# Two halves for projections and four-tile turns on TensorE in an attention and expert kernel

## The chip, the cores and the metric

The kernel runs on one core of a Trainium2 chip. The metric is device time in microseconds (us) for one execution, the median of several runs. TensorE's queue is called PE below, its weight loads PEld, VectorE DVE, ScalarE ACT, GpSimd POOL and SyncE SP. ACTq and SPq are rows of DMAs that those two queues issue.

## The reference, cut to what matters

```python
# x: 16 batches x 512 tokens x 128 channels; 16 heads of 8 channels
h = layernorm(x) * (1 + ca) + sa
Q, K, V = h @ Wq.T, h @ Wk.T, h @ Wv.T      # reshaped to (16 heads, batch, 512, 8) over the flat data
atten = softmax(Q K^T)                       # 512 x 512 for each batch and head
y = atten V + h
x = x + ga * (y - mean(y)) / sqrt(var(y) + eps)      # mean and variance over a whole batch
h = layernorm(x) * (1 + cb) + sb
x = x + gb * experts(h)                      # 8 experts of 128 -> 256 -> 128, the best two by a gate
```

## The kernel before, in words

Attention comes first, in 17 stages (`over_stages`), then the expert layer, batch by batch (`f_batch`). Each engine has its own instruction queue with the order written out by hand, and the queues meet on semaphores.

A stage has 16 quads (`r`), each with four heads (`h`). In a quad PE issues, for each head, one score matmul of pass A (`pass_a`, L1135, keys across a row, for the row maxima) and one of pass B (`pass_b`, L1147, transposed scores, for the exponentials); A and B of one head lie on different halves of the array's rows and run as a pair. The quad ends with the value matmuls (`values`, L1160, eight instructions, since each f32 matmul is issued as two). Pass A runs on batch b. Pass B and the values run 13 quads (`LAG`) behind it, so that in the first 13 quads of stage b they work on batch b-1. DVE takes the row maxima of pass A (L716), ACT the exponentials of pass B (L985). Passes A and B have three PSUM banks each: a pass-A matmul waits for the maximum three before it, a pass-B matmul for the exponential three before it.

One more PSUM bank, `misc`, serves all the other work on PE, one use after the other. `misc_uses(b)` lists by quad what stage b does there: quad 0 the turn (transpose) of the next batch's normed input (`x_turn`), quad 1 the row maxima of the batch before (`max_rows`), quads 2, 3 and 4 the next batch's projections `q`, `k`, `v`, quads 8 to 10 two one-column matmuls and another `max_rows`, quad 15 the turn of an earlier batch's result (`z_turn`). PE does such a use in `fill`, behind the second head (`h == 1`) of the quad: it waits on `s_misc_read` until the use before has been read, issues the matmuls, and counts up `s_misc_full`. ACT reads the bank (`evacuate`: L932 hT, L937 q_f, L941 k_f, L945 v_f, L949 max_rows) before the exponentials of the next quad; DVE reads `z_turn` (L763) behind the maxima of quad 15. In quad 2, ACT also issues three DMAs between its second and third exponential (`halfway`: two at L974, one at L999).

The projections go through memory before the next stage can use them. POOL splits q_f, then k_f, into three bf16 parts (lines 339 to 345). SP, in a fixed order, stores q (L373) and v (L382), loads Qt (L393), stores k (L378), loads v (L421) and loads Kt (L411). The first pass-A matmul of the next stage waits on `s_q_landed` and `s_k_landed`.

Stage 0 has pass A alone in its first 13 quads. Stages 0 to 14 do x_turn, q, k and v for the next batch; stages 2 to 16 do z_turn. Stage 16 has no pass A. Before stage 0 the first batch's four fills run by themselves, and the last batch's end is done among the experts (`end_piece`).

Of the kernel before, what the change touches and what calls it, by code (L numbers as in the profile page):

```python
# [15 lines left out]
P = 128  # L16
# [18 lines left out]
TT = S // P  # L35
# [27 lines left out]
def misc_index(what, b, g=0):  # L63

    return MISC[(what, b, g)]
# [7 lines left out]
def build(nc, x, wqT, wkT, wvT, w1, b1T, w2, b2T, w3, b3, gate_w, cT, wmod, out):  # L73
    ctx = ExitStack()
    with ctx:
        def sb(name, shape, dt=F32):
            return ctx.enter_context(nc.sbuf_tensor(name, shape, dt))

        def sem(name):
            return ctx.enter_context(nc.semaphore(name))  # L80
# [49 lines left out]
        hT = sb("hT", [P, S])  # L130
# [77 lines left out]
        misc = bank[7]  # L208
        misc_bf = misc[:].bitcast(BF16)

        def end_bank(b):

            return pv_bank if isinstance(b, int) and b == NB - 1 else misc
# [21 lines left out]
        s_misc_full = sem("s_misc_full")  # L235
# [86 lines left out]
        def has(b, first, last):  # L322

            return not isinstance(b, int) or first <= b <= last
# [756 lines left out]
        def _(pe):  # L1081
# [4 lines left out]
            for j in range(6):  # L1086
                ins = pe.matmul(misc[:, j * NB:(j + 1) * NB], wmod_sb[:, j], c_silu[:], start=True, stop=True)
# [2 lines left out]
            pe.transpose(misc[0:NB, 0:D], mod[:, 5], ident[:]).then_inc(s_gb_mm, 1)  # L1090
            pe.wait_ge(s_gb, 1)

            def fill(what, b, g=0):

                n = misc_index(what, b, g)
                if n:
                    pe.wait_ge(s_misc_read, n)
                if what == "x_turn":
                    pe.wait_ge(s_x_norm, TT * (b + 1))
                    for t in range(TT):  # L1100
                        ins = pe.transpose(misc[:, P * t:P * t + P], x_norm[:, t], ident[:])
                if what in ("q", "k"):
                    w = wq_sb if what == "q" else wk_sb
                    ins = pe.matmul(misc[:], w[:], hT[:], start=True, stop=True)  # L1104
                if what == "v":
                    for t in range(TT):
                        ins = pe.matmul(misc[:, P * t:P * t + P], hT[:, P * t:P * t + P], wv_sb[:],  # L1107
                                        start=True, stop=True)
                if what == "max_rows":
                    pe.wait_ge(s_split_max[3], 2 * b + g + 1)  # L1110
                    ins = pe.transpose(misc_bf[0:PARTS * MCOLS, 0:P], max_parts[:].rearrange("p a i n -> p (a i n)"),
                                       ident_bf[:])
                if what == "mean":
                    pe.wait_ge(s_y_mv, b + 1)
                    ins = pe.matmul(end_bank(b)[:, 0:1], mean_mat[:], y_mv[:, 0:1], start=True, stop=True)
                if what == "var":
                    pe.wait_ge(s_y_sq, b + 1)
                    ins = pe.matmul(end_bank(b)[:, 0:1], mean_mat[:], y_sq[:], start=True, stop=True)
                if what == "z_turn":
                    pe.wait_ge(s_z, b + 1)  # L1120
                    for t in range(TT):
                        ins = pe.transpose(end_bank(b)[:, P * t:P * t + P], z[:, P * t:P * t + P], ident[:])
                ins.then_inc(s_misc_full, 1)

            def pass_a(b, r, h):
                g, c = r // 4, r % 4
                a, n = head(g, h)
                first = HALF * a
                m = b * STEPS + 4 * r + h
                if r + h == 0:  # L1130
                    pe.wait_ge(s_q_landed, (b + 1) * LOADS * DMA)
                    pe.wait_ge(s_k_landed, (b + 1) * LOADS * DMA)
                if m >= 3:
                    pe.wait_ge(s_max, m - 2)
                pe.matmul(score_a[m % 3][:], Qt[b % BUFS][first:first + ROWS, n, P * c:P * c + P],  # L1135
                          Kt[b % BUFS][first:first + ROWS, n], start=True, stop=True).then_inc(s_a, 1)
# [58 lines left out]
            def stage(b, par):  # L1195
                for r in range(QUADS):
                    for h in range(4):
                        if has(b, 0, NB - 1):
                            pass_a(b, r, h)
                        if r < LAG and has(b, 1, NB):  # L1200
                            pass_b(b - 1, r + QUADS - LAG, h)
                        if r >= LAG and has(b, 0, NB - 1):
                            pass_b(b, r - LAG, h)
                        if h == 1:
                            for q, what, ub, g in misc_uses(b):
                                if q == r:
                                    fill(what, ub, g)
                    if r <= LAG and has(b, 1, NB):
                        values(b - 1, 1 - par, r + QUADS - LAG - 1)
                    if r > LAG and has(b, 0, NB - 1):  # L1210
                        values(b, par, r - LAG - 1)
                    if b_is(b, NB) and 1 <= r <= E:
                        f_piece(0, 0, r - 1)
# [84 lines left out]
```

## Time and profile before

| | |
|---|---|
| median of 3 runs | 1527.62 us (1523.94 to 1529.97) |
| profiled execution, its own time | 1535.74 us |
| its span | 1533.9 us |
| mean granted TensorE clock, share of full speed | 0.973 |
| busy: PE, DVE, ACT, POOL | 88%, 75%, 56%, 18% |
| stage 0, from its first pass A | 52.1 to 98.6 us |
| stages 1 to 14 | 98.6 to 808.1 us |
| stages 15 and 16 | 808.1 us to about 893 us |
| experts | from about 893 us |

All rows come from one execution. A start in a row is in us from the span's start. The idle time in brackets is what the engine spent before that instruction, and the name behind the arrow is the inferred releaser; "issue" means that the profile shows none, which is also what a wait for a DMA can look like. Matmuls overlap, so their step is read from one start to the next and not from the duration.

### The profile page before, as it was taken

To read this page: it belongs to the slowest core of one execution; us is meant where nothing else is said; L and a number is where in the kernel's file an instruction comes from. 1 tells how busy PE (TensorE), PEld (TensorE's weight loads), DVE (VectorE), ACT (ScalarE), POOL (GpSimd) and SP (SyncE) were. 2 spreads that over 40 slices of the span, in tenths; PEclk is the share of its full clock that TensorE was granted. 3 is DMA by queue.
4 is the path that set the end of the run, shared out by engine and by line. 5 is a ranking of instruction groups with operands and counts; after the bars stand their busy time and mean duration, and the time that the engine had idled before them with its cause. 6 is when DMAs were issued, how large, how long until landed. Compare 5 with 4: busy or idle time off the path is not lost.

```text
span 1533.9 us, 24345 instructions
## 1 busy us (share of the span) xinstructions
PE 1355.0 (88%) x8445; PEld 735.2 (48%) x8445; DVE 1151.3 (75%) x2821; ACT 855.6 (56%) x1590; POOL 279.8 (18%) x411
## 2 busy tenths in 40 slices
PE   2697888888878888888888899999999999999998
PEld 1121222122212222222221258888888888888887
DVE  4587888898888888887898437766676766677775
ACT  2067787788887787877787753333333333333332
POOL 3221332233213331332121111000000000000000
PEclk9999999999999999999999799999999999999999
DMA  8346465556555565646552210000000000000000
GB/s 157 78 76 121 89 127 116 105 119 128 121 112 122 116 131 114 118 107 125 110 112 64 75 44 23 16 16 17 16 16 16 16 16 16 17 16 14 11 11 13
DMA packets 355834, 108.93 MB, mean 71 GB/s; under 512 B 282448, under 2 KB 338176, under 8 KB 352640
## 3 DMA queue, kind: packets, MB, share of 16 engines
q1 hardware_dynamic: 343232, 89.81, 29.9%
q10 hardware_dynamic: 12480, 17.57, 3.8%
q8 instruction: 67, 1.10, 0.3%
q14 instruction: 55, 0.45, 0.1%
HBM read 59.88 MB, written 46.67 MB: 69 GB/s over the span
## 4 chain that ended last, share of the span: by engine, by line
PE 65%; DVE 18%; ACT 9%; issue 4%; ACTq 3%; DMA 1%; SPq 1%; POOL 0%; POOLq 0%; DVEq 0%
PE bank L1231 22%; PE bank L1243 15%; DVE neg_max L716 14%; PE bank L1160 10%; PE bank L1135 7%; ACT probs L985 5%; PE bank L1147 4%; ACTq L974 2%; PE bank L1104 2%; PE bank L1107 1%; DMA Kt<-k_dram 1%; PE bank L1191 1%; ACTq L999 1%; PE bank L1180 1%; ACT x_norm L959 1%
## 5 line engine op out<-in xcount | busy, mean ns | idle before, releaser
L716 DVE TENSOR_REDUCE neg_max<-bank 128x1 f32<-128x512 f32 x1024 | 638.3, 682 | 134.3 <-PE bank L1135 132.0
L985 ACT ACTIVATE probs<-bank 128x512 f32<-128x512 f32 x1024 | 539.7, 603 | 165.9 <-PE bank L1147 156.1
L1135 PE MATMUL bank<-Kt,Qt 48*128 48x512 bf16 x1024 | 346.5, 407 | 105.3 <-DVE neg_max L716 56.6
L1231 PE MATMUL bank<-h_part,w_parts 128*128 128x512 f32 x1536 | 384.3, 399 | 3.3 <-DVE hidden L881 3.3
L1066 ACT ACTIVATE gate_act<-bank,b_sb 128x512 f32<-128x512 f32 x256 | 176.4, 689 | 373.8 <-PE bank L1231 373.7
L1147 PE MATMUL bank<-Qt,Kt 51*128 51x512 bf16 x1024 | 339.4, 401 | 25.1 <-ACT probs L985 24.0
L1231 PEld LDWEIGHTS bank<-h_part,w_parts 128*128 128x128 f32 x1536 | 278.2, 188 | 64.8 <-DVE hidden L881 10.2
L881 DVE SCALAR_TENSOR_TENSOR hidden<-bank,b_sb,gate_act 128x512 f32<-128x512 f32 x256 | 190.7, 750 | 136.9 <-ACT gate_act L1066 136.4
L1135 PEld LDWEIGHTS bank<-Kt,Qt 48*128 48x128 bf16 x1024 | 73.9, 95 | 455.9 <-DVE neg_max L716 364.2
L1160 PE MATMUL bank<-probs,Vt 128*16 128x512 f32 x2048 | 282.2, 624 | 0.1
L1243 PEld LDWEIGHTS bank<-w_sb,hidden 128*128 128x128 f32 x2048 | 247.1, 192 | 8.9
L1243 PE MATMUL bank<-w_sb,hidden 128*128 128x128 f32 x2048 | 249.0, 275 | 0.0
L892 DVE SCALAR_TENSOR_TENSOR acc<-bank,w_dense,acc 128x128 f32<-128x128 f32 x512 | 144.0, 344 | 45.0 <-PE bank L1243 44.9
L1147 PEld LDWEIGHTS bank<-Qt,Kt 51*128 51x128 bf16 x1024 | 73.0, 94 | 70.2 <-ACT probs L985 67.6
L648 POOL TENSOR_TENSOR y_out<-acc,gb_all 128x512 f32<-128x512 f32 x16 | 20.6, 1289 | 445.9 <-DVE acc L892 445.9
L1160 PEld LDWEIGHTS bank<-probs,Vt 128*16 128x16 f32 x2048 | 33.6, 95 | 76.0 <-issue 50.9
L339 POOL CAST max_parts<-neg_max 128x32 bf16<-128x32 f32 x32 | 6.8, 211 | 311.3 <-DVE neg_max L716 311.3
L994 ACT ACTIVATE o_sb<-bank 128x512 f32<-128x512 f32 x64 | 38.2, 597 | 12.9 <-PE bank L1160 12.0
L339 POOL CAST q_parts<-q_f 128x512 bf16<-128x512 f32 x15 | 9.2, 616 | 146.6 <-ACT q_f L937 146.6
L610 POOL TENSOR_TENSOR f_rstd<-f_ve,neg_half 128x4 f32<-128x4 f32 x16 | 16.3, 1016 | 98.6 <-DVE f_ve L690 98.6
L959 ACT ACTIVATE x_norm<-x_in,x_shift,x_rstd 128x128 f32<-128x128 f32 x64 | 27.9, 492 | 10.9 <-DVE x_shift L702 10.9
L586 POOL TENSOR_TENSOR x_rstd<-x_ve,neg_half 128x4 f32<-128x4 f32 x16 | 16.3, 1020 | 90.2 <-DVE x_ve L690 90.2
(123 smaller groups left out, 797.7 us busy)
## 6 DMA issues: line engine op xcount, KB each, us to landing
o_dram<-o_sb ACTq DMA_DIRECT2D x64, 256.0 KB, 3.9
q_dram<-q_parts SPq DMA_DIRECT2D x48, 128.0 KB, 4.5
k_dram<-k_parts SPq DMA_DIRECT2D x48, 128.0 KB, 11.6
Qt<-q_dram SPq DMA_DIRECT2D x32, 192.0 KB
Kt<-k_dram SPq DMA_DIRECT2D x32, 192.0 KB
x_in<-in_x SPq DMA_DIRECT2D x16, 256.0 KB, 3.1
h_dram<-hT SPq DMA_DIRECT2D x16, 256.0 KB, 3.7
Qt<-q_dram SPq DMA_DIRECT2D x32, 128.0 KB
```

The lines of the kernel that those rows point to most:

```text
L716: dve.tensor_reduce(neg_max[:, side, a, col:col + 1], score_a[m % 3][:], AX_X, ALU.max, negate=True).then_inc(s_max, 1)
L881: dve.scalar_tensor_tensor(hidden[slot], up_bank[2 * c + 1][:], b2_sb[:, c, e:e + 1], gate_act[:, c], ALU.add, ALU.mult).then_inc(s_hid, 1)
L892: ins = dve.scalar_tensor_tensor(acc[:, par, t], down_bank[e % 2][:, P * t:P * t + P], w_dense[par][:, t, e:e + 1], acc[:, par, t], ALU.mu ...
L959: act.activation(x_norm[:, t], x_in[:, t], ACT.Identity, bias=x_shift[:, t:t + 1], scale=x_rstd[:, t:t + 1]).then_inc(s_x_norm, 1)
L985: act.activation(probs[:, 4 * (j % 2) + (k ^ 1)], score_b[n % 3][:], ACT.Exp).then_inc(s_exp, 1)
L994: act.activation(o_sb[:, g % 2], pv_bank[:], ACT.Copy).then_inc(s_o, 1)
L1066: act.activation(gate_act[:, c], up_bank[2 * c][:], ACT.Silu, bias=b1_sb[:, c, e:e + 1])\
L1135: pe.matmul(score_a[m % 3][:], Qt[b % BUFS][first:first + ROWS, n, P * c:P * c + P], Kt[b % BUFS][first:first + ROWS, n], start=True, stop ...
L1147: pe.matmul(score_b[m % 3][:], Kt[b % BUFS][first:first + ROWS + PARTS, n, P * c:P * c + P], Qt[b % BUFS][first:first + ROWS + PARTS, n], ...
L1160: ins = pe.matmul(pv_bank[32 * h:32 * h + 2 * DK, :], Vt[:, par, 4 * (N8 * a + n) + c], probs[:, 4 * (j % 2) + h], start=(c == 0), stop=(c ...
L1231: ins = pe.matmul(up_bank[2 * c + k][:], w[:, i, e, P * c:P * c + P], h_parts[par][j], start=(i + j == 0), stop=(i == 1))
L1243: ins = pe.matmul(down_bank[e % 2][:, P * t:P * t + P], hidden[HC * (e % 2) + c][:, P * t:P * t + P], w3_sb[:, e, c], start=(c == 0), stop ...
```

## The change

`fill` gets a parameter `half`. For x_turn, q, k, v and z_turn (`h_turn` is named too and is no use of this kernel) it is called twice: behind the quad's second head with half 0, and behind its fourth head, ahead of the value matmuls, with half 1. A half is two of the four tiles, or 256 of the 512 columns of the q and k projections. The wait on `s_misc_read` stands in front of the first half only and `s_misc_full` is counted behind the second half only. The waits for the normed input and for z stand in front of both. `max_rows` and the one-column matmuls stay whole, and calls outside the stages have no halves.

```diff
+            def in_two(what):
+                return what in ("x_turn", "q", "k", "v", "z_turn", "h_turn")
+
-            def fill(what, b, g=0):
+            def fill(what, b, g=0, half=None):
 
+                tiles = range(TT) if half is None else range(TT // 2 * half, TT // 2 * (half + 1))
+                columns = slice(P * tiles[0], P * tiles[-1] + P)
                 n = misc_index(what, b, g)
-                if n:
+                if n and not half:
                     pe.wait_ge(s_misc_read, n)
                 if what == "x_turn":
                     pe.wait_ge(s_x_norm, TT * (b + 1))
-                    for t in range(TT):
+                    for t in tiles:
                         ins = pe.transpose(misc[:, P * t:P * t + P], x_norm[:, t], ident[:])
                 if what in ("q", "k"):
                     w = wq_sb if what == "q" else wk_sb
-                    ins = pe.matmul(misc[:], w[:], hT[:], start=True, stop=True)
+                    ins = pe.matmul(misc[:, columns], w[:], hT[:, columns], start=True, stop=True)
                 if what == "v":
-                    for t in range(TT):
+                    for t in tiles:
                         ins = pe.matmul(misc[:, P * t:P * t + P], hT[:, P * t:P * t + P], wv_sb[:],
                                         start=True, stop=True)
...
-                    for t in range(TT):
+                    for t in tiles:
                         ins = pe.transpose(end_bank(b)[:, P * t:P * t + P], z[:, P * t:P * t + P], ident[:])
-                ins.then_inc(s_misc_full, 1)
+                if half != 0:
+                    ins.then_inc(s_misc_full, 1)
...
-                        if h == 1:
+                        if h in (1, 3):
                             for q, what, ub, g in misc_uses(b):
-                                if q == r:
+                                if q == r and in_two(what):
+                                    fill(what, ub, g, h // 2)
+                                elif q == r and h == 1:
                                     fill(what, ub, g)
```

## Rows read from the trace of the kernel before

**Rows 1.** Timeline of PE, first pass A of four stages: start, us, line [idle].
```profile
403.18 0.37 PE L1135 MATMUL bank<-Kt,Qt 48*128 48x512 bf16 x1 [1.05 <-issue]
...
602.73 0.37 PE L1135 MATMUL bank<-Kt,Qt 48*128 48x512 bf16 x1 [1.66 <-issue]
...
652.73 0.37 PE L1135 MATMUL bank<-Kt,Qt 48*128 48x512 bf16 x1 [1.89 <-issue]
...
705.01 0.58 PE L1135 MATMUL bank<-Kt,Qt 48*128 48x512 bf16 x1 [2.34 <-issue]
```
**Rows 2.** Windows: stretch, us, then PE, PEld, DVE, ACT, POOL busy, PEclk, DMA share, GB/s.
```profile
96.00:97.00 1.00, 1.00 (x6) 0.15 (x2) 0.50 (x1) 0.40 (x1) 0.00 (x0) 1.00 0.24 40
...
402.00:403.00 1.00, 0.13 (x4) 0.00 (x0) 0.85 (x2) 0.17 (x1) 0.53 (x3) 1.00 0.35 88
403.00:404.00 1.00, 0.82 (x7) 0.43 (x8) 0.34 (x1) 0.32 (x1) 0.92 (x3) 1.00 0.01 2
```
**Rows 3.** Timeline of the SP queue in the stage that began at 602.73.
```profile
616.60 3.28 SPq L373 DMA_DIRECT2D q_dram<-q_parts  x3
...
643.18 2.14 SPq L411 DMA_DIRECT2D Kt<-k_dram  x6
```
**Rows 4.** Timeline of ACT, the reading of q in three of those stages.
```profile
412.31 0.60 ACT L937 ACTIVATE q_f<-bank 128x512 f32<-128x512 f32 x1
...
612.14 0.60 ACT L937 ACTIVATE q_f<-bank 128x512 f32<-128x512 f32 x1
...
663.97 0.60 ACT L937 ACTIVATE q_f<-bank 128x512 f32<-128x512 f32 x1
```
**Rows 5.** Timeline of all engines, quads 0 to 2 of the stage that began at 403.18.
```profile
403.68 2.17 ACT L985 ACTIVATE probs<-bank 128x512 f32<-128x512 f32 x4 [1.52 <-PE bank L1147]
...
405.74 0.78 ACT L932 ACTIVATE hT<-bank,mod 128x512 f32<-128x512 f32 x1
...
406.06 0.38 PE L1135 MATMUL bank<-Kt,Qt 48*128 48x512 bf16 x1
...
406.40 2.07 ACT L985 ACTIVATE probs<-bank 128x512 f32<-128x512 f32 x4
...
406.57 0.12 PEld L1111 LDWEIGHTS bank<-ident_bf,max_parts 128*96 128x96 bf16 x1 [0.63 <-ACT hT L932]
...
408.99 0.26 ACT L949 ACTIVATE max_rows<-bank 96x128 bf16<-96x128 bf16 x1
...
410.85 0.44 ACTq L999 DMA_DIRECT2D o_dram<-o_sb  x1
...
411.34 1.09 ACT L985 ACTIVATE probs<-bank 128x512 f32<-128x512 f32 x2 [1.11 <-PE bank L1147]
```
**Rows 6.** Groups by line and form, 300 to 800 us: count, busy us, mean ns.
```profile
L1104 PE MATMUL bank<-hT,wq_sb 128*128 128x512 f32 x20 | 11.3, 644 | 3.4 <-ACT max_rows L949 3.4
```
**Rows 7.** Windows, four us from the start of two of the stages (columns of Rows 2).
```profile
652.73:656.73 4.00, 4.00 (x20) 0.96 (x20) 2.58 (x4) 2.84 (x5) 0.00 (x1) 0.59 0.06 8
...
403.18:407.18 4.00, 3.86 (x29) 1.33 (x29) 3.41 (x6) 3.50 (x7) 0.80 (x2) 1.00 0.08 12
```
**Rows 8.** Timeline of stage 0, quad 2, the q projection.
```profile
58.00 2.07 PE L1104 MATMUL bank<-hT,wq_sb 128*128 128x512 f32 x2
...
60.64 2.48 DVE L716 TENSOR_REDUCE neg_max<-bank 128x1 f32<-128x512 f32 x4 [1.44 <-PE bank L1135]
```
**Rows 9.** Timeline of PE, second head of quad 4 up to the values.
```profile
720.17 0.38 PE L1135 MATMUL bank<-Kt,Qt 48*128 48x512 bf16 x1
720.50 1.16 PE L1107 MATMUL bank<-wv_sb,hT 128*128 128x128 f32 x8
721.59 0.39 PE L1135 MATMUL bank<-Kt,Qt 48*128 48x512 bf16 x1
...
721.82 0.38 PE L1135 MATMUL bank<-Kt,Qt 48*128 48x512 bf16 x1
722.13 1.05 PE L1160 MATMUL bank<-probs,Vt 128*16 128x512 f32 x8
```

## The prediction

> **What bounds the kernel now.** I read the page's chain of waits first. PE holds most of it, which is misleading: shares are an average over stages, and the question is what releases the first instruction of each stage. So next come the starts of the stages on PE. Each of the four shown has PE idle for 1.05 to 2.34 us in front of its first pass A, with no releaser named [rows 1]; ten of the fifteen starts from stage 1 on have such a gap, 0.41 to 5.61 us long. What PE waits for shows in the windows around 403.18: DMA traffic falls from a share of 0.35 to 0.01 just as PE starts [rows 2]. The last transfers then under way are the Kt loads. In the stage that began at 602.73 SP has issued the last of them at 643.18 + 2.14 = 645.32, and the next stage begins at 652.73 [rows 1, 3], 7.4 us later; over the starts with a gap this is 6.4 to 8.4 us.
>
> So a stage ends when its K has landed. I follow that back. The splitting, the stores, the loads and the landing hang in one chain behind ACT's reading of q: q_f at 612.14, q store at 616.60, Kt issued by 645.32, next start at 652.73, with the k stores between [rows 1, 3, 4]. From q_f to the next start that is 40.6 us; for the stage that began at 652.73 it is 705.01 - 663.97 = 41.0 us. Over the starts of stages 2 to 15 it stays within 39.7 to 42.1, whatever PE did meanwhile. Even the four starts without a gap lie at 40.4 to 40.9, so PE and the landing come in together there. **A stage lasts the time from its start to q_f, plus about 40.7 us.** The second term holds none of the moved instructions. The first is 412.31 - 403.18 = 9.13 us, 612.14 - 602.73 = 9.41, and 663.97 - 652.73 = 11.24 [rows 1, 4]. The longest one began at 1.2 GHz: the granted clock is 0.59 over its first four us, against 1.00 at 403.18 [rows 7].
>
> What fills the 9.13 us? Exponentials of quad 0, then hT at 405.74. The max_rows turn of quad 1 is released by hT, at 406.57. Behind it come the values of quad 1, the copy of the output bank and max_rows at 408.99. Then ACT goes through quad 2 at its own pace, with three DMA issues, up to the third exponential at 411.34 and q_f at 412.31 [rows 4, 5].
>
> **Part 1, the cost of the halves themselves.** The trace shows no 256-column f32 projection. One of 512 columns takes two instructions, 11.3 us for ten, 1.13 us each [rows 6]. The v projection is the same number of columns in eight instructions of 128, and from its start at 720.50 to the next pass A at 721.59 it takes 1.09 us [rows 9]. Cut four times finer, it costs no more. So two halves cost 1.13 us together: I take 0 extra; the bounds are -0.04 and, if a half paid as much as the whole, +1.13 us.
>
> What does come new is one more turn-round of the array. A pair to the next pair is 721.82 - 721.59 = 0.23 us; a pair to a full-array matmul is 720.50 - 720.17 = 0.33, and a pair to the values 722.13 - 721.82 = 0.31 [rows 9]. So leaving the pairs costs 0.08 to 0.10 us. That is paid before the fill and before the values now, and will be paid before half 0 and before half 1: the same count. New is half 1 to the values, full array to four column strips. I take 0.05 us, between 0 and 0.10. The trace has no such sequence. The Trainium skill, "TensorEngine Tiling (Array Packing)", Key Properties, says that a change of tiling mode drains the TensorE, and that speaks against the change, which has one more of them per fill. By it the value would be at the upper end, 0.10; the sum below would grow by 0.7 us.
>
> **Part 2, quads 2 to 4 and 15 in stages 1 to 14.** In quads 2 to 4 the second and third pairs' products reach DVE and ACT half a fill (0.56 us) sooner, and the values begin where they did. PE itself finishes these quads no sooner: all its matmuls are still there, and the stall ahead of k is for q_f, which ACT reads no sooner than its DMA issues allow (the third exponential follows the last issue, 410.85 + 0.44 = 411.29, by 0.05 us [rows 5]). k_f comes some 0.6 us sooner, and POOL is then still splitting q. v_f comes some 0.4 us sooner, and SP is still issuing the q store (3.3 us [rows 3]). Both gains end there. So does the cost of 0.05 us each: the cover is the gap before the next start [rows 1]. In the four stages without a gap the cover is thin and up to four turn-rounds may count: 4 x 4 x 0.05 = 0.8 at most, of which I take 0.2 us, since DVE, not PE, paces quads 5 to 13. For z_turn, DVE reads the bank behind its last maximum, which is after half 1 as well.
>
> **Part 3, quad 0 in stages 1 to 14, the one on the path.** Half of x_turn leaves from in front of the third pass B. Where the stage starts at full clock the four exponentials take 2.17 us [rows 5]; four that wait for nothing take 2.07, as those at 406.40 do. So ACT waits only 0.10 us there, and that is the gain for hT. hT also needs half 1, which ends at about 404.9, ahead of 405.6. From hT it goes on to max_rows, whose weights wait for it: the last pair is at 406.06, would let it start at 406.06 + 0.33 = 406.39, and it starts at 406.57 [rows 5, 9]. So 0.18 us can be won at most, and ACT gives 0.10. The turn-round of 0.05 lies in that slack. Nine such stages: -0.9 us. Where the stage starts at 1.2 GHz, PE is the later one (its max_rows turn follows the pair at once) and the turn-round counts, at half clock doubled: 5 x 0.1 = +0.5 us.
>
> **Part 4, stage 0.** No exponentials there. The q fill takes 2.07 us, and DVE stands idle for 1.44 us behind it [rows 8]. With halves, DVE gets two more products between them, but PE's total for a quad with a fill, 3.9 us, stays above DVE's 2.5, so PE paces quads 2 to 4 either way. Only the last half of the run overlaps better: about -0.3 us. ACT reads q behind half 1, so q_f is later by two pass A, 0.9 us. This costs nothing as long as K is early: DMA traffic is down to a share of 0.24 in the window from 96 us [rows 2], 1.6 us and more ahead of the start at 98.6, and what moves after it is the next x_in. Bounds: -1.5 (DVE's idle time at the first q fill gone) to +0.9 us (q_f decides).
>
> **The sum.** -0.9 + 0.5 - 0.3 + 0.2 = -0.5 us against the profiled execution's 1535.74 (span 1533.9 and 1.8 around it): 1535.2. That execution lies 8.1 us above the median of the runs and above all three, so I carry the difference over: 1527.62 - 0.5, about **1527.1 us**. The experts, from 893 us on, are not touched.
>
> **Rivals.**
> *Slower: the starts go cold.* Moving work about changes how busy PE is at the ends of stages. The starts at 403.18 and 602.73, after gaps of 1.05 and 1.66 us, ran on at full clock; those at 652.73 and 705.01, after 1.89 and 2.34, fell to 1.2 GHz [rows 1, 7]. A cold start costs 11.24 - 9.27 (mean of 9.13 and 9.41) = 2.0 us and is on the path. It needs gaps that grow by 0.3 us or so in the nine full-clock stages. Against it: the path through PE keeps its length, so the gaps should too. One to three more cold starts: 1529 to 1533 us, chance 0.12. Four or more make it over 0.5% slower; five would give 1527.1 + 10 = 1537 us, chance 0.09.
> *Slower: the turn-rounds decide.* If PE and not K ended the stages, five turn-rounds of 0.10 us in 14 stages would add 7 us: 1534 us. It is also where a half that costs more than half would show: 0.2 us more per x_turn is 2.8 us. The steady 40.7 us from q_f to the start speaks against it. Chance 0.04.
> *Faster: q comes sooner.* The profile names pass B as releaser of the third exponential in quad 2 (1.11 us [rows 5]). If that were so, halving the q fill would give ACT the product 0.56 us sooner and q_f with it: 14 x 0.5 = 7 us, 1520 us. Against it: the wait ends 0.05 us behind ACT's own DMA issues. Chance 0.07.
> *Faster: cold starts go warm.* Five stages pay 0.7 to 2.5 us for theirs. Without them it would be 1527.1 - 10 = 1517 us. For it: PE's work is spread more evenly in the quad with z_turn, just ahead of the start. Against: it is the same work, and the gap for K stays. Chance 0.06.
> *It does nothing at all* is my forecast to within 1 us, and cannot be told from it by time; the traces would tell.
>
> **How the numbers follow.** Forecast 0.62, its own range 1523.5 to 1530 (the runs before spread that much). About 0.5%, 7.6 us, is what a measurement of this kernel can tell from no change. Faster by more: 0.06 + 0.06 (of the 0.07) = 0.12. Slower by more: 0.09 + 0.02 (of the 0.04) = 0.11. Within: 0.77. The range for 8 in 10 takes in one to three more cold starts, and on the other side the case with q sooner: 1520 to 1534 us.
>
> **What would show it.** Right: first pass A behind a gap with DMA traffic ending there, 40 to 41 us from q_f to it, 9.0 to 9.4 us from a start at full clock to q_f, the third exponential of quad 2 still on the heels of L999, k_f half a microsecond earlier. Step 1 is wrong if the two halves' q matmuls sum to more than 1.13 us or the values start later than 0.33 us behind half 1's last matmul. Part 3 is wrong if hT moves by 0.5 us. The whole is wrong if stages no longer end with K, or if the count of stages beginning at 1.2 GHz changes by four.

## The result

The changed kernel takes 1538.43 us (median of 20 runs, 1532.22 to 1551.5), the one of before 1532.41 us in the same comparison (20 runs, 1523.67 to 1541.62). The ratio is 1.0047, interval 1.0025 to 1.0069: some 7 us slower. I had forecast no change (-0.5 us) and a range that ended at 1534.

The profiled execution hides this. It took 1532.61 us, with a span of 1530.8 us, less than the 1533.9 us profiled before; it is the second quickest of the 20. The 20 runs spread over 19 us for the change and over 18 us for the kernel of before, and over all runs of this study the time follows the mean granted TensorE clock closely: 0.96 us for each 0.001 of it, with one slope for all kernels and an offset for each. So a single trace can't show the loss as a sum; it shows mechanisms. Medians of several rounds show the sum, and below I add for each kernel its difference to before at the same clock (least squares over 278 runs, +- is one standard error). The ratios in the tables are against the runs of before in the same rounds and leave out the few executions more than 1.5% above the fastest of their kernel, so they are not always the quotient of the two medians shown.

Where the two profiles differ is not where the change sits. From the first pass A of stage 1 to that of stage 15 both take 709.6 us (98.56 to 808.13 before, 98.64 to 808.22 after). Stage 0 took 1.0 us more, the time ahead of it 0.9 us less, and the part behind 808 us took 3.2 us less, with a higher granted clock in stages 15 and 16. Windows, before and then after (stretch, us, PE, PEld, DVE, ACT, POOL busy, PEclk, DMA share, GB/s):
```profile
808.13:900.00 91.87, 80.14 (x456) 19.50 (x456) 52.08 (x127) 66.72 (x131) 9.31 (x17) 0.84 0.21 59
```
```profile
808.22:900.00 91.78, 77.38 (x465) 20.39 (x466) 52.87 (x128) 69.10 (x134) 9.31 (x17) 0.91 0.22 62
```

Page of after, header and the chain that ended last:
```profile
span 1530.8 us, 24465 instructions
PE 66%; DVE 18%; ACT 7%; issue 3%; ACTq 3%; DMA 1%; SPq 1%; POOL 0%; POOLq 0%; DVEq 0%
```

Timeline of PE in after, first pass A of four stages (L1141 there, L1135 before; the answer to [rows 1]):
```profile
98.64 0.37 PE L1141 MATMUL bank<-Kt,Qt 48*128 48x512 bf16 x1 [2.17 <-issue]
...
301.72 0.37 PE L1141 MATMUL bank<-Kt,Qt 48*128 48x512 bf16 x1 [0.96 <-issue]
...
400.60 0.37 PE L1141 MATMUL bank<-Kt,Qt 48*128 48x512 bf16 x1
...
451.49 0.61 PE L1141 MATMUL bank<-Kt,Qt 48*128 48x512 bf16 x1
```
The row at 400.60 has no bracket: PE came straight from the values. Of the fifteen starts from stage 1 on, five have a gap; before it was ten. **PE used up the wait for K.** From q_f to the next start it is now 41.3 to 41.7 us in seven of fourteen stages, where 40.7 had been usual; six of these seven lead to a start without a gap.

Quads 0 to 3 of the stage at 400.60, all engines, cut to the moved work. It answers to [rows 5] and [rows 9]:
```profile
401.14 0.44 PE L1106 MATMUL bank<-ident,x_norm 128*128 128x128 f32 x2
...
401.51 0.39 PE L1141 MATMUL bank<-Kt,Qt 48*128 48x512 bf16 x1
...
401.82 0.39 PE L1141 MATMUL bank<-Kt,Qt 48*128 48x512 bf16 x1
...
402.14 0.44 PE L1106 MATMUL bank<-ident,x_norm 128*128 128x128 f32 x2
...
402.51 1.05 PE L1166 MATMUL bank<-probs,Vt 128*16 128x512 f32 x8
403.03 0.80 ACT L932 ACTIVATE hT<-bank,mod 128x512 f32<-128x512 f32 x1
...
406.60 0.26 ACT L949 ACTIVATE max_rows<-bank 96x128 bf16<-96x128 bf16 x1
...
406.91 0.70 PE L1109 MATMUL bank<-hT,wq_sb 128*128 128x256 f32 x2 [0.34 <-ACT max_rows L949]
...
407.55 0.39 PE L1141 MATMUL bank<-Kt,Qt 48*128 48x512 bf16 x1
...
408.08 0.70 PE L1109 MATMUL bank<-hT,wq_sb 128*128 128x256 f32 x2
...
408.71 1.05 PE L1166 MATMUL bank<-probs,Vt 128*16 128x512 f32 x8
...
409.92 0.60 ACT L937 ACTIVATE q_f<-bank 128x512 f32<-128x512 f32 x1
```
Half of q takes 407.55 - 406.91 = 0.64 us, and the other half 408.71 - 408.08 = 0.63, together 1.27. A whole q took 410.37 - 409.31 = 1.06 before:
```profile
409.31 1.12 PE L1104 MATMUL bank<-hT,wq_sb 128*128 128x512 f32 x2 [0.34 <-ACT max_rows L949]
410.37 0.39 PE L1135 MATMUL bank<-Kt,Qt 48*128 48x512 bf16 x1
```
Half of x_turn takes 0.37 us twice, a whole one 0.59. So a further burst costs some 0.2 us. And hT is sooner, as forecast, at 2.43 us behind the start instead of 2.56; but max_rows is at 6.00 instead of 5.81, and q_f at 9.32 instead of 9.13.

### The profile page after: what moved, and what is told of

Read it like the earlier page. It is cut to its first block, busy times and chain, and to the rows that moved or that the text cites. A ratio compares the mean times of both kernels' runs of the same rounds, so it can differ in the third digit from the quotient of the medians.

```text
span 1530.8 us, 24465 instructions
## 1 busy us (share of the span) xinstructions
PE 1366.8 (89%) x8505; PEld 741.8 (48%) x8505; DVE 1149.7 (75%) x2821; ACT 856.8 (56%) x1590; POOL 279.6 (18%) x411
## 4 chain that ended last, share of the span: by engine, by line
PE 66%; DVE 18%; ACT 7%; issue 3%; ACTq 3%; DMA 1%; SPq 1%; POOL 0%; POOLq 0%; DVEq 0%
PE bank L1239 22%; PE bank L1251 15%; DVE neg_max L716 15%; PE bank L1166 10%; PE bank L1141 8%; ACT probs L985 4%; PE bank L1153 3%; PE bank L1109 2%; ACTq L974 2%; PE bank L1112 1%; PE bank L1197 1%; PE bank L1127 1%; ACTq L999 1%; DMA Kt<-k_dram 1%; PE bank L1106 1%
## 5 line engine op out<-in xcount | busy, mean ns | idle before, releaser
L1141 PE MATMUL bank<-Kt,Qt 48*128 48x512 bf16 x1024 | 347.8, 407 | 93.6 <-DVE neg_max L716 56.6
L1141 PEld LDWEIGHTS bank<-Kt,Qt 48*128 48x128 bf16 x1024 | 74.1, 95 | 434.3 <-DVE neg_max L716 351.8
## 6 DMA issues: line engine op xcount, KB each, us to landing
k_dram<-k_parts SPq DMA_DIRECT2D x48, 128.0 KB, 11.7
```

## The experiments

Each kernel was run beside the one of before. Nothing of the computation is left out in this table.

| kernel | runs | median us | ratio (95% interval) | mean granted clock | vs before at the same clock, us |
|---|---|---|---|---|---|
| before | 103 | 1531.81 | 1 | 0.9738 | 0 |
| the change | 20 | 1538.43 | 1.0047 (1.0025 to 1.0069) | 0.9711 | +4.2 +- 0.6 |
| e1 both halves behind the second head | 12 | 1529.28 | 0.9976 (0.9943 to 1.0008) | 0.9756 | -1.4 +- 0.7 |
| e2 x_turn alone in halves | 12 | 1531.32 | 0.9986 (0.9953 to 1.0019) | 0.9749 | +0.2 +- 0.7 |
| e3 q, k, v alone | 12 | 1533.61 | 0.9996 (0.9964 to 1.0029) | 0.9767 | +3.4 +- 0.7 |
| e12 z_turn alone | 12 | 1534.66 | 1.0005 (0.9971 to 1.0038) | 0.9698 | -1.3 +- 0.7 |
| e4 whole fills in front of the values | 12 | 1544.54 | 1.0064 (1.0029 to 1.0099) | 0.9712 | +8.2 +- 0.7 |
| e5 quarters | 6 | 1585.33 | 1.0348 (1.0316 to 1.0381) | 0.9668 | +46.3 +- 1.0 |
| e8 output stores a quad later | 12 | 1541.27 | 1.0057 (1.0033 to 1.0081) | 0.9680 | +3.2 +- 0.7 |
| e16 longer, whole fills | 9 | 1541.71 | 1.0075 (1.0047 to 1.0102) | 0.9666 | +2.4 +- 0.8 |

Without K's way through memory from the fourth batch on (each stage then ends when PE does):

| kernel | runs | median us | ratio to before | mean granted clock | a stage at full clock, us |
|---|---|---|---|---|---|
| e6 whole fills | 6 | 1510.34 | 0.9856 (0.9817 to 0.9895) | 0.9790 | 48.0 |
| e9 x_turn in halves | 6 | 1507.71 | 0.9846 (0.9811 to 0.9881) | 0.9820 | 48.15 |
| e10 q, k, v | 6 | 1516.28 | 0.9902 (0.987 to 0.9935) | 0.9798 | 48.4 |
| e11 z_turn | 6 | 1513.80 | 0.9890 (0.9862 to 0.9918) | 0.9775 | 48.1 |
| e14 x_turn, q, k, v | 8 | 1519.41 | 0.9920 (0.989 to 0.995) | 0.9775 | 48.5 |
| e15 q, k, v, z_turn | 12 | 1534.29 | 1.0000 (0.9968 to 1.0032) | 0.9670 | 48.45 |
| e7 all five | 12 | 1532.04 | 1.0002 (0.9979 to 1.0024) | 0.9682 | 48.7 |
| e13 longer, whole fills | 12 | 1524.97 | 0.9952 (0.9931 to 0.9972) | 0.9739 | 48.7 |

### What a half costs: e1, e5, e4

e1 leaves the cut and takes away the second place:
```diff
-                        if h in (1, 3):
+                        if h == 1:
                             for q, what, ub, g in misc_uses(b):
                                 if q == r and in_two(what):
-                                    fill(what, ub, g, h // 2)
+                                    fill(what, ub, g, 0)
+                                    fill(what, ub, g, 1)
```


> All five fills cut in two as in the change, but both halves stand behind the second head, one right after the other. In the change, a half of q takes 0.63 us from its start to the next pass A and a whole one of before 1.05 to 1.06, so two halves cost 0.21 us more than the whole; v and x_turn cost 0.19 and 0.16 more. Theory A (a fixed price per burst of full-array matmuls among the pairs and values, about 0.2 us, paid once more when the fill is broken in two places): adjacent halves cost what the whole costs, q 1.06 us (up to 1.10), gaps ahead of the stages as before, ratio 1.000 (0.998 to 1.002). Theory B (the price lies in the shorter matmuls and the second loading of q's and k's weights): q takes 1.26 us here too, v and x_turn stay at 1.09 and 0.58, ratio about 1.002.

Timeline of PE in e1, the q projection (four instructions, both halves):
```profile
306.10 1.13 PE L1109 MATMUL bank<-hT,wq_sb 128*128 128x256 f32 x4 [0.34 <-ACT max_rows L949]
307.17 0.39 PE L1141 MATMUL bank<-Kt,Qt 48*128 48x512 bf16 x1
```
1.07 us for two halves in one place. Shorter matmuls and the second loading of the weights cost nothing that shows; a second place costs 0.2 us. Theory A.

e5 puts one quarter behind each head:
```diff
-                tiles = range(TT) if half is None else range(TT // 2 * half, TT // 2 * (half + 1))
+                tiles = range(TT) if half is None else range(half, half + 1)
...
-                if half != 0:
+                if half is None or half == 3:
...
-                        if h in (1, 3):
-                            for q, what, ub, g in misc_uses(b):
-                                if q == r and in_two(what):
-                                    fill(what, ub, g, h // 2)
+                        for q, what, ub, g in misc_uses(b):
+                            if q == r and in_two(what):
+                                fill(what, ub, g, h)
```


> Every one of the five fills in four quarters, one behind each head. Theory A (each further burst costs PE about 0.2 us at full clock): three more bursts per fill instead of one, so q takes 1.05 + 0.6 us in all, PE loses 5 x 3 x 0.2 = 3.0 us per stage, 42 us in 14 stages; the gap ahead of the stages (mean 1.2 us before) swallows at most 1.2 x 14 = 17 us of it, none is left, and the time grows by 25 to 35 us, ratio 1.016 to 1.023. If DVE's waits cover part of it in quads 13 to 15 and 0, 15 us remain, 1.010. Rival (the change's loss came from TensorE's clock and cutting costs next to nothing, 0.05 us a burst): below 10 us.

Timeline of PE in e5, three of q's quarters:
```profile
109.40 0.49 PE L1109 MATMUL bank<-hT,wq_sb 128*128 128x128 f32 x2
109.82 0.39 PE L1141 MATMUL bank<-Kt,Qt 48*128 48x512 bf16 x1
...
110.14 0.49 PE L1109 MATMUL bank<-hT,wq_sb 128*128 128x128 f32 x2
110.56 0.39 PE L1141 MATMUL bank<-Kt,Qt 48*128 48x512 bf16 x1
...
110.88 0.49 PE L1109 MATMUL bank<-hT,wq_sb 128*128 128x128 f32 x2
111.30 1.05 PE L1166 MATMUL bank<-probs,Vt 128*16 128x512 f32 x8
```
A quarter takes 0.42 us. Whole 1.06, half 0.63, quarter 0.42: that is 0.21 us fixed and 0.85 us by columns, with one line through all three. It is the same before a pair (bf16) as before the values (f32), 0.42 both, so a change of number format is not what costs. The total was beyond what I expected: 53 us, or 0.25 us for each of the 15 x 14 further bursts (46 us or 0.22 at the same clock), with hardly any hidden by gaps.

e4 tells the place from the cut:
```diff
-                                if q == r and in_two(what):
-                                    fill(what, ub, g, h // 2)
-                                elif q == r and h == 1:
+                                if q == r and h == (3 if in_two(what) else 1):
                                     fill(what, ub, g)
```


> The five fills whole, but behind the fourth head, in front of the values, instead of behind the second. This tells the place from the cut. Theory A (price per burst): a whole fill here costs PE no more than before, q about 1.05 us from its start to the values, and no stage loses more than 0.1 us on PE; hT, which now waits for the whole turn behind the fourth pair, still comes after the fourth exponential, so q_f keeps 9.1 us; stage 0 loses about 1 us; ratio 1.000 to 1.001. Rival (it is the place in front of the values that costs, because the values must wait for an f32 fill): the time is that of the change, 1.004 to 1.005, and gaps vanish as there.

Against my expectation it is not as fast as before, and at the same clock it is 4 us slower than the change (the intervals of the two ratios overlap). Timelines of DVE and PE in e4, quads 3 and 4 (the PE rows are quad 3):
```profile
414.43 2.48 DVE L716 TENSOR_REDUCE neg_max<-bank 128x1 f32<-128x512 f32 x4 [1.05 <-PE bank L1141]
418.04 2.48 DVE L716 TENSOR_REDUCE neg_max<-bank 128x1 f32<-128x512 f32 x4 [1.13 <-PE bank L1141]
```
```profile
415.18 0.39 PE L1141 MATMUL bank<-Kt,Qt 48*128 48x512 bf16 x1 [0.35 <-DVE neg_max L716]
415.26 0.39 PE L1153 MATMUL bank<-Qt,Kt 51*128 51x512 bf16 x1
415.58 1.13 PE L1109 MATMUL bank<-hT,wk_sb 128*128 128x512 f32 x2
416.63 1.05 PE L1166 MATMUL bank<-probs,Vt 128*16 128x512 f32 x8
```
The fill itself is at its old price (1.05 us up to the values). But fill and values in one block, 2.04 us, last longer than the three products that DVE has in hand: it stands idle for 1.1 us ahead of such a quad, and then PE waits 0.35 us for DVE at the fourth pair. Between 300 and 800 us DVE's idle time ahead of its maxima grew from 66.6 to 75.6 us, and the time that PE's pass A waits for DVE from 35.4 to 51.4. So the work between the heads does have a use, which is to keep DVE fed. Two other losses stand beside it and were not separated from it: q_f came 9.5 us or more behind every start at full clock, where before and in my expectation it was 9.1 or more, and stage 0 lasted 48.2 us instead of 46.5.

### Which part loses: e2, e3, e12

The list in `in_two` is cut to x_turn, to q, k and v, or to z_turn.

> Only x_turn in two halves (quad 0), q, k, v and z_turn whole. Theory A with K's landing as the bound: x_turn's extra 0.16 us and its later third pair lie on the way to q_f, which comes 9.3 us behind a start at full clock instead of 9.1; the way from q_f to the next start stays 40.7 us on average, and gaps like those of before (0.4 to 3.5 us, in about ten of fifteen) remain. 14 x 0.2 = 2.8 us, ratio 1.002. Rival (PE itself ends the stages, and only the sum of fill prices counts): 14 x 0.16 = 2.2 us but gaps smaller by as much. Rival (the time lost in the change is all from TensorE's clock): ratio 1.000, unless the mean granted clock falls.

> Only q, k and v in two halves, x_turn and z_turn whole. Theory A: q_f comes 9.1 us behind a start at full clock, as before; PE loses 3 x 0.2 = 0.6 us in quads 2 to 4, which goes on through the stage and shrinks the gaps from a mean near 1.2 to about 0.6 us. Where a gap is left nothing is lost; where none was, 0.6 us: 4 to 8 stages, 2.4 to 4.8 us, ratio 1.002 to 1.003. Rival (K alone bounds the stages): ratio 1.000. Rival (clock): follows the mean granted clock only, 1 us for each 0.001 of it.

> With K again, only z_turn in halves, the one part not yet timed alone. x_turn alone gave 0.9986 (0.9953 to 1.0019), q, k and v alone 0.9996 (0.9964 to 1.0029), all five 1.0047. If the parts add up, z_turn alone is the one that costs: 1.004 to 1.006. If they do not (each alone fits into the gap ahead of the next stage, 1.2 us on average, all together at 1.0 us do not where the gap is small): 1.000 to 1.001, gaps as before.

In e2 q_f comes 9.34 us behind a start at full clock, as expected, and the time does not show it: 1.0019 is the upper end, my 1.002 just beyond. In e3 q_f comes at 9.10, gaps are left at all but one of the fifteen starts, and at the same clock 3.4 us are lost, which is within 2.4 to 4.8; but the ratio can't tell it from nothing. e12 tells nothing from zero either. By the ratios no part alone shows a loss, and the interval of q, k and v (up to 1.0029) still touches that of the change (from 1.0025). At the same clock 3.4 +- 0.7 us beside 4.2 +- 0.6 says that most of the direct loss is that of q, k and v.

### Who ends a stage: e6, e7, e8

e6 and e7 take K's traffic away from the kernel of before and from the changed one. From the fourth batch on they leave out K's stores and loads and score with old keys; the engines' work is the same.
```diff
-                if what == "k":
+                if what == "k" and b < BUFS:
                     sp.wait_ge(s_split_k[3], b + 1)
...
             def k_load(b):
 
+                if b >= BUFS:
+                    return
...
-                pe.wait_ge(s_k_landed, (b + 1) * LOADS * DMA)
+                pe.wait_ge(s_k_landed, min(b + 1, BUFS) * LOADS * DMA)
```


> The kernel of before, but from the fourth batch on K is neither stored to memory nor loaded again (36 of 45 stores, 72 of 90 loads less; the result is wrong from there, the work of the engines is the same). If K's landing ends the stages, they now end with PE: no gaps, and 12 stages get shorter by the mean gap of 1.2 us and by what cold starts after gaps cost: 15 to 25 us faster, ratio 0.984 to 0.990, warm stages of 47.9 us instead of 48.9 to 50. If K's landing was never the bound: ratio 1.000 and the gaps stay.

> The same omission in the changed kernel. Nothing but PE, DVE and ACT end a stage then, so the difference to the same omission in the kernel of before is the bare price of the halves: theory A 5 x 0.2 us in 14 stages = 14 us (12 to 16), less what DVE covers in quads 13 to 15; a warm stage lasts 48.9 instead of 47.9 us. In the change itself the gaps hid the larger part. Rival (gaps hid nothing and the direct cost is the 4 us seen at equal clock): the difference between the two omissions is 4 us.

Without K's traffic the kernel of before gains 22 us, as expected: K's landing does end most of its stages. The changed one gains 6 us on its own 1538: PE already ended most of its stages. The bare difference of the halves is 1532.0 - 1510.3 = 21.7 us, more than the 14 of theory A and far more than 4. Stages at full clock last 48.0 us (642.12 to 690.15) and 48.7 us (204.16 to 252.86), so the work itself explains 0.7 x 14 = 10 us. The five prices read from starts add up to 0.9 us; what covers the other 0.2 was not measured. The rest goes with the clock, 0.0108 lower at 0.96 us for each 0.001. Timelines of PE in e6 and then e7, starts of two stages in a row:
```profile
642.12 0.39 PE L1137 MATMUL bank<-Kt,Qt 48*128 48x512 bf16 x1
...
690.15 0.39 PE L1137 MATMUL bank<-Kt,Qt 48*128 48x512 bf16 x1
```
```profile
508.59 0.60 PE L1143 MATMUL bank<-Kt,Qt 48*128 48x512 bf16 x1
...
559.90 0.60 PE L1143 MATMUL bank<-Kt,Qt 48*128 48x512 bf16 x1
```
The pass A of 0.60 us in e7 runs at 1.2 GHz, and that stage lasts 51.31 us. In e7's profile six stages in a row last 51.25 to 51.37 us, each with its slow stretch at the same place: the stretches begin 51.2 us apart, which is as long as a stage with such a stretch lasts. Windows across the end of a stage, e6 and then e7 (stretch, us, PE, PEld, DVE, ACT, POOL busy, PEclk, DMA share, GB/s):
```profile
392.00:396.00 4.00, 2.54 (x17) 0.75 (x18) 2.45 (x5) 4.00 (x10) 0.00 (x0) 1.00 0.19 68
396.00:400.00 4.00, 3.75 (x32) 1.24 (x33) 4.00 (x8) 3.29 (x8) 1.46 (x5) 1.00 0.35 54
```
```profile
398.00:402.00 4.00, 2.63 (x14) 0.45 (x14) 2.23 (x5) 4.00 (x10) 0.00 (x0) 0.88 0.19 68
402.00:406.00 4.00, 4.00 (x18) 0.86 (x16) 2.88 (x5) 1.99 (x4) 1.14 (x5) 0.50 0.19 30
406.00:410.00 4.00, 4.00 (x28) 1.00 (x24) 2.58 (x4) 2.84 (x5) 0.33 (x1) 0.77 0.84 200
```
Both have the same weak spot ahead of it. In quad 14 PE waits 1.18 us for an exponential, behind ACT's x_norm and z. In e6 the clock held through it here, in e7 it fell. It is no mark of the halves: five other stages of e6 last 49.2 to 49.5 us and have a slow stretch behind the same wait, and all 23 slow stretches between 290 and 760 us in the profiles of e6, e7 and e15 begin 0.0 to 1.6 us behind the matmul that waited so.
```profile
393.85 0.39 PE L1149 MATMUL bank<-Qt,Kt 51*128 51x512 bf16 x1 [1.18 <-ACT probs L987]
```
```profile
399.76 0.39 PE L1155 MATMUL bank<-Qt,Kt 51*128 51x512 bf16 x1 [1.18 <-ACT probs L987]
```

e8 tries to use the bound: q_f sooner, in the kernel of before.
```diff
-                    done = r - 1 + QUADS - LAG
-                    if 1 <= r <= LAG + 1 and done % 4 == 0 and has(b, 1, NB):
+                    done = r - 2 + QUADS - LAG
+                    if 2 <= r <= LAG + 2 and done % 4 == 0 and has(b, 1, NB):
                         o_store(b - 1, done // 4 - 1)
```


> The kernel of before with whole fills; ACT issues the store of each output group (L999) one quad later, so in quad 2 it stands no longer between the second and the third exponential, and q_f can come 0.5 us sooner (8.6 instead of 9.1 us behind a start at full clock; up to 1.3 us sooner where that issue took 1.29 us). If q_f to K's landing is the path of the stages with a gap: ten or eleven stages gain 0.5 us until PE ends them, 3 to 6 us faster, ratio 0.996 to 0.998, gaps 0.5 us smaller. If q_f is not on the path: 1.000. If pass B's third product and not ACT's issues released the third exponential: q_f stays at 9.1.

Timeline of ACT and SP in e8, the stage that began at 667.88:
```profile
674.76 0.73 ACTq L974 DMA_DIRECT2D Qt<-max_rows  x1
675.54 1.08 ACT L985 ACTIVATE probs<-bank 128x512 f32<-128x512 f32 x2 [0.60 <-PE bank L1147]
676.51 0.60 ACT L937 ACTIVATE q_f<-bank 128x512 f32<-128x512 f32 x1
```
```profile
670.30 2.42 SPq L435 DMA_DIRECT2D den<-o_dram  x4
...
682.46 0.54 SPq L452 DMA_DIRECT2D den_inv<-inv_dram  x1
683.04 3.49 SPq L373 DMA_DIRECT2D q_dram<-q_parts  x3
```
q_f comes at 8.63 us: the third exponential was indeed released by ACT's own DMA issues. Yet the kernel is slower. The last store of a batch now lands later, SP's loads of it begin at 670.30 instead of right behind the start, the whole list on SP shifts, and the q store waits behind den_inv until 683.04, 6.5 us behind q_f instead of 4.5. I had moved a DMA without asking what is queued behind its landing. The gaps grew (38.7 us in the profile against 21.0 before), and the granted clock fell to 0.968.

### Why the parts do not add up: e9 to e11, e13 to e16

The parts without K's traffic (e9 x_turn, e10 q, k and v, e11 z_turn):

> K neither stored nor loaded from the fourth batch on (as in the two runs before this), only x_turn in halves. Whole fills gave 1510.3 us, all halves 1532.0 without K: 21.7 us, of which the warm stages (48.0 and 48.7 us in the profiles) explain 0.7 x 14 = 10, and the rest goes with a granted clock of 0.968 against 0.979. Theory A (bare prices add up, the clock is an even tax on all of it): x_turn has 0.2 of 1.0 us, so 4 us of the 22, 1514 us. Theory B (the chill comes from the turns around the stage's end, the bursts next to quad 14's idle 1.2 us on PE): 6 to 8 us, clock 0.974 or less.

> The same without K, only q, k and v in halves. Theory A: 0.6 of 1.0 us, 13 us, 1523 us, clock about 0.973; warm stages 48.4 to 48.6 us. Theory B: the bare 0.4 to 0.6 us per stage only, 6 to 8 us, 1517 us, clock 0.978 as with whole fills.

> The same without K, only z_turn in halves. Theory A: 0.16 of 1.0 us, 3.5 us, 1514 us. Theory B: z_turn stands in quad 15, right behind the idle time of quad 14, and brings most of the chill: 8 us or more, clock 0.972 or less.

-2.6, +5.9 and +3.5 us against e6, 6.8 together, where all five cost 21.7. These are medians of six runs, each difference uncertain by 3 to 4 us (one standard error) and their sum by some 10, so this alone shows little. At full clock the stages add up (0.15 + 0.4 + 0.1 against 0.7 us). The clock doesn't: 0.982, 0.980, 0.978 alone, 0.968 together. Pairs, and a stage that is longer for another reason:

> Without K traffic, x_turn, q, k and v in halves, z_turn whole. If z_turn's halves are needed for the chill: 1516 to 1520 us, clock 0.978. If length decides (48.5 to 48.6 us warm): between, 1518 to 1528 us.

> Without K traffic, q, k, v and z_turn in halves, x_turn whole. If z_turn together with the longer stage makes the chill: 1525 to 1532 us, clock 0.970. If all five are needed, or x_turn's halves: 1516 to 1520 us, clock 0.978.

```diff
-                    for t in range(TT):
+                    for t in (0, 1) * (b > 0) + tuple(range(TT)):
                         ins = pe.transpose(misc[:, P * t:P * t + P], x_norm[:, t], ident[:])
...
-                    for t in range(TT):
+                    for t in (0, 1, 2) * (b > 0) + tuple(range(TT)):
                         ins = pe.matmul(misc[:, P * t:P * t + P], hT[:, P * t:P * t + P], wv_sb[:],
```


> Without K traffic, whole fills behind the second head, but v computes three of its four tiles twice and x_turn two of its four (the same values again): 0.75 + 0.2 us more on PE per stage, no further burst; a warm stage should last about 48.6 to 48.8 us, as with all halves. If the cold spells follow from the length of the stage by whatever means: clock about 0.968 to 0.972 and 1525 to 1532 us. If they come from the halves themselves: 10 us for the bare work and the clock stays at 0.979, 1520 us.

> With K traffic, whole fills with the same repeated tiles. If the change's 0.47% is nothing but PE being longer by some 0.7 us per stage, wherever it comes from, this gives the same: ratio 1.003 to 1.006. If the places of the bursts matter: 1.000 to 1.002, as the gaps hide 0.7 us in most stages.

q, k, v with z_turn already have the whole effect (1534.3 us, clock 0.967); with x_turn instead they don't (1519.4, 0.978). This step is clear of the noise: 15 us between the two, and 15 us more than the sum of what q, k, v and z_turn cost alone. One of e15's twelve runs took 1514.83 us at a clock of 0.982, ten between 1532.8 and 1538.5 at 0.962 to 0.967. So the same program has a way through with few slow stretches, at about 1515 us, and one with a slow stretch in nearly every stage, 20 us longer. In e15's profile the two stages from 201.84 on last 48.5 us each, the next 50.4, and then eight in a row 51.1 to 51.8 us; e7's leaves the rhythm for one stage at 661.94 and falls back.

e13 has the same length of stage and not the rhythm. It costs 14.6 us over e6, and its mean clock of 0.974 looks like a loss of clock; the windows say otherwise. Stretches of e13 and then e6 and e7 (columns as above):
```profile
74.00:101.20 27.20, 25.90 (x68) 4.38 (x67) 25.46 (x51) 9.47 (x18) 2.10 (x6) 0.50 0.50 92
101.50:798.40 696.90, 602.41 (x4058) 159.19 (x4056) 602.49 (x1168) 559.40 (x1101) 185.47 (x302) 0.98 0.40 95
```
```profile
74.00:99.60 25.60, 24.40 (x65) 4.12 (x65) 23.99 (x48) 9.47 (x18) 1.96 (x6) 1.00 0.55 97
99.64:784.80 685.16, 589.38 (x3942) 145.94 (x3942) 601.74 (x1168) 559.14 (x1101) 185.97 (x303) 0.98 0.42 96
```
```profile
101.20:809.00 707.80, 618.93 (x3998) 154.36 (x3998) 601.79 (x1169) 560.91 (x1101) 185.04 (x298) 0.95 0.40 93
```
In stages 1 to 14 e13 keeps e6's clock of 0.98 and is 11.7 us longer, 10 of them by work; e7 has 0.95 there. What lowers e13's mean clock is one spell of 27 us at 1.2 GHz in stage 0, 0.009 of the whole run. It costs little: DVE is busy for 25.46 of its 27.20 us and sets the pace, and stage 0 lasts 49.1 us against 47.0, repeated tiles included. Eight of e13's twelve runs have a clock about 0.009 lower than the other four at like times, so most seem to have had it. So the length of a stage does not bring the rhythm on; the halves of q, k, v together with z_turn's do. Why this pair falls into it is left open: the runs show that it does, not what decides.

With K's traffic e16 costs 1.0075, no less than the change (1.0047; the intervals overlap) and more than I expected. So PE being 0.7 us longer per stage, with no further burst, is sufficient for a loss of the change's size. It need not be made up the same way: e16's profile has the same 27 us at 1.2 GHz in stage 0, which lasts 48.4 us against 46.5, and seven of its nine runs have the lower clock of such a spell. That makes the +2.4 us at the same clock in the table too small; with 0.009 given back to those runs it is about +9 us (an estimate), at a mean clock equal to that of before, where the change has 4.2 us and a lower clock.

## Why the prediction was wrong

Two steps failed: the price of a second burst (Part 1), taken at a quarter of what it is, and the cover for it (Part 2), taken to be the gap ahead of the next start in nearly every stage.

**What bounds the kernel: right, but read as a licence.** K's landing ends most stages (e6: 22 us without it). From q_f to the next start it is less steady than I wrote: the four starts of before without a gap lie at 40.1 to 41.0 us, not 40.4 to 40.9, and the changed kernel's starts behind a gap, from stage 2 on, at 40.0 to 41.7. I took the mean of the gaps as cover for PE. Six of the fifteen starts had 0.41 us or none. And a gap of 1 to 2 us is not spare in a kernel whose PE runs slow for a while in many stages: with a slow stretch the same work took 49.5 us instead of 48.0 in e6 and 51.3 instead of 48.7 in e7, and the gap had been paying for it.

**Part 1, a half's price: the term that was mis-sized.** I took 0.05 us, with 0.10 as the upper end. It is 0.2 us: 0.21 for q and k, 0.19 for v, 0.16 for x_turn. The sign that I had named for it came: the halves of q sum to 1.27 us, more than 1.13. I had priced the turn-round from the pairs into the fill (0.33 - 0.23 us, [rows 9]) and not the one out of it, because I read v's 1.09 us as eight times a column price and saw that q costs the same. A fixed part can't be seen in two whole fills of equal length; it takes two bursts of one kind and unequal length, as the halves and quarters then were (x_turn: 0.59 us for four turns, 0.37 for two). The rule of the Trainium skill that I put beside it ("TensorEngine Tiling (Array Packing)", Key Properties: a change of tiling mode drains the TensorE) pointed the right way; the trace agrees in that going in and out once more costs 0.2 us. That a drain is what takes this time no run shows.

**Part 2: the sum per stage.** I counted a part of 0.2 us for all stages together. Measured bare, PE's stage is 0.7 us longer, 10 us in all (e7 against e6). With K's traffic 3 to 4 us of loss are left at an equal clock (the change +4.2 +- 0.6, e3 +3.4 +- 0.7). k_f came 2.72 us behind q_f instead of 3.15: sooner, by 0.43 and not 0.6 us, and worth nothing, as said.

**Part 3: right in its first step, wrong in sign.** hT gained 0.13 us against 0.10 forecast. But the second burst and the fourth pair, which now waits for DVE (401.51 to 401.82, 0.31 instead of 0.23 us), put PE behind ACT: max_rows lost 0.19 us instead of gaining 0.10. The slack of 0.18 us that I named was smaller than this. I also miscounted the starts of stages 1 to 14: eight at full clock and six slow ones, not nine and five, which makes the term -0.2 instead of -0.4.

**Part 4: wrong in its reason.** q_f of stage 0 came 0.58 us later (8.60 against 8.02), not 0.9. The start at 98.64 has a gap of 2.17 us, so K ended stage 0 in that execution, where I had it early. The rows of before could have told: the last Kt issue of stage 0 ended at 91.68, 6.9 us ahead of the start at 98.56, within the 6.4 to 8.4 us that I had read for starts with a gap. What the halves cost there stays open: stage 0 lasts 47.4 us against 46.5 before, but 47.4 in e1 too, whose order is the old one. The window that I read for it, 96 to 97 us [rows 2], is no proof that the last load has landed.

**The rivals.** "The turn-rounds decide" had the mechanism, at 0.10 us and a chance of 0.04. "The starts go cold" had the other part, though not by its count: seven of the fifteen starts begin at a lowered clock in both profiles. I tied it to growing gaps, from rows that left out the start at 453.04, which had a gap of 2.00 us and ran on at full clock. The loss came with vanishing gaps: in stages 1 to 14 ten of the changed kernel's eleven slow stretches begin while PE works toward the end of a stage, against six of ten before, and now little or no gap covers them. On average over runs the change has 2.7 thousandths less clock, 2.6 +- 1.1 us, beside the 4.2 us at equal clock. "q comes sooner" is refuted by e8's trace, and by that of the change: with the halved fill the third exponential still starts 0.05 us behind ACT's last issue.

**The level.** Three runs of before, median 1527.62, set my zero; 103 runs give 1531.8. With a right -0.5 us the range would have held 1531 as well. The upper end of 1534 failed by 4 us, about that error of the level; the sign and the size of the change failed by Part 1 and its cover.

No version here beats the kernel of before beyond its interval. e1, the same order with finer instructions, has the lowest median of those that compute everything (0.9976, up to 1.0008).

## What to carry to other kernels

Breaking one burst of full-array matmuls into two among packed ones had a fixed price here, 0.16 to 0.21 us for each further burst; get it from two bursts of unequal length before trusting a price per column. A gap in front of a stage is no free cover: count the stages where it is nearly nothing, and what else it absorbs, such as slow stretches of TensorE. Where time follows the granted clock from run to run, compare many runs and look at the clock beside each median; one profile can have the wrong sign, as here. And ask where the clock was lost: 27 us at half clock lowered the mean of e13 by 0.009 and cost it at most 2 us, since DVE set the pace there.

## What the runs showed of the hardware

A program can run in two rhythms: e15's twelve runs took 1514.83 us at a granted clock of 0.982 or 1532.8 us and more at 0.962 to 0.967 (but for one at 1525.35 and 0.972), and in the slow rhythm of e15's and e7's profiles the stretch at 1.2 GHz came at the same place in each stage, behind a PE wait of 1.18 us. And a matmul that waits for DMA can show "issue" as releaser with no DMA named, as at all ten starts with a gap before; the DMA share of 1-us windows (0.35, then 0.01) told which it was.
